# First maxima between the quarters of a feature product, and their rows sent from two queues among the last stores

## What is computed

```python
q = (x @ Wq).reshape(b, n, NUM_KV_GROUPS, GROUP_SIZE, HEAD_DIM)
k = (x @ Wk).reshape(b, n, NUM_KV_GROUPS, HEAD_DIM)
v = (x @ Wv).reshape(b, n, NUM_KV_GROUPS, HEAD_DIM)
scores = jnp.einsum('bqgsd,bkgd->bgsqk', q, k) * scale
scores = jnp.where(causal, -jnp.inf, scores)
attn = jax.nn.softmax(scores, axis=-1)
ctx = jnp.einsum('bgsqk,bkgd->bqgsd', attn, v)
```

## Time and profile before

| | |
|---|---|
| median of the runs before | 2528.2 us (2526.11 to 2528.24, 3 runs) |
| the profiled execution's own time | 2528.26 us |
| its span, first to last instruction | 2526.5 us |
| PE busy | 2413.8 us (96%) |
| DVE busy | 1737.0 us (69%) |
| ACT busy | 1426.1 us (56%) |
| POOL busy | 1610.2 us (64%) |
| mean granted PE clock | 0.972 |

### The profile page before, as it was taken

The page is one execution under the profiler, slowest core; times in us unless marked ns, Lnnn a source line. Parts: engine busy times, 40 slices in busy tenths (PEclk is TensorE's granted clock), DMA queues, the critical chain, the costliest instruction groups (busy, mean ns, idle before and its releaser), DMA issues. The chain is left out here.

```text
span 2526.5 us, 38828 instructions
## 1 busy us (share of the span) xinstructions
PE 2413.8 (96%) x12834; PEld 1726.7 (68%) x12834; DVE 1737.0 (69%) x3804; ACT 1426.1 (56%) x2761; POOL 1610.2 (64%) x1751
## 2 busy tenths in 40 slices
PE   8979999999999999996979999999999997999998
PEld 6865555555555555544767888887888885788886
DVE  3358778888888888833876655666656564877776
ACT  3215556666666666663865555666656554454553
POOL 4404577777877767776957667675576765555554
PEclk9999899999999999998989999999999998999999
DMA  7853655574656566555964545466445457674553
GB/s 248 270 169 84 132 124 125 115 151 113 145 112 145 118 144 123 116 107 157 355 202 138 166 137 159 145 217 186 152 141 160 132 164 245 189 226 131 148 151 102
DMA packets 249177, 400.87 MB, mean 159 GB/s; under 512 B 57712, under 2 KB 112016, under 8 KB 237584
## 3 DMA queue, kind: packets, MB, share of 16 engines
q1 hardware_dynamic: 196000, 283.48, 36.8%
q0 software_dynamic: 52480, 114.37, 20.5%
q10 hardware_dynamic: 496, 0.54, 0.1%
HBM read 180.63 MB, written 112.22 MB: 116 GB/s over the span
## 5 line engine op out<-in xcount | busy, mean ns | idle before, releaser
L1142 ACT ACTIVATE p_probs<-p_ps_s 128x512 f32<-128x512 f32 (+3 forms) x1280 | 591.1, 541 | 327.0 <-PE p_ps_s L1060 310.1
L1727 POOL DMA_DIRECT2D p_eT<-p_ex x1024 | 538.4, 535 | 272.9 <-DVE p_ex L1993 220.4
L1169 DVE TENSOR_REDUCE p_parts<-p_ps_m 128x1 f32<-128x512 f32 x752 | 459.1, 681 | 82.9 <-PE p_ps_m L1045 74.6
L1060 PE MATMUL p_ps_s<-q,k_e 98*128 98x512 f32 (+3 forms) x1280 | 468.4, 387 | 3.5 <-ACT p_probs L1142 3.1
L1045 PE MATMUL p_ps_m<-k_m,q 96*128 96x512 f32 (+2 forms) x1232 | 434.6, 387 | 11.9 <-PEq L2268 10.2
L981 POOL TENSOR_TENSOR p_added<-p_added,p_probs 128x2048 f32<-128x2048 f32 x88 | 419.4, 4769 | 34.5 <-ACT p_probs L1142 17.0
L1060 PEld LDWEIGHTS p_ps_s<-q,k_e 98*128 98x128 f32 x1280 | 241.8, 191 | 183.6 <-ACT p_probs L1142 76.3
L1078 PE MATMUL p_ps_c<-p_probs,v_e 128*32 128x512 f32 (+3 forms) x2560 | 285.3, 547 | 10.0 <-POOL p_probs L961 10.0
L1045 PEld LDWEIGHTS p_ps_m<-k_m,q 96*128 96x128 f32 x1232 | 235.4, 194 | 86.4 <-DVE p_parts L1173 20.2
L2127 POOL TENSOR_TENSOR p_acc<-p_acc,logit 128x512 f32<-128x512 f32 x112 | 162.5, 1451 | 153.6 <-ACT logit L2180 150.1
L1173 DVE CUSTOM_DVE_ANT_0 p_masked<-p_ps_m,p_mask 128x128 f32<-128x128 f32 (+1 forms) x480 | 203.9, 485 | 25.7 <-PE p_ps_m L1045 25.6
(11 more groups left out here) (204 smaller groups left out, 4979.4 us busy)
## 6 DMA issues: line engine op xcount, KB each, us to landing
p_probs<-p_probs POOLq DMA_DIRECT2D x56, 1024.0 KB, 7.9
logits_t<-logit SPq DMA_DIRECT2D x32, 1024.0 KB, 5.0
p_eT<-p_ex POOLq DMA_DIRECT2D x1024, 32.0 KB, 2.1
logit<-logits_t SPq DMA_DIRECT2D x128, 256.0 KB, 3.5
q<-q_t SPq DMA_DIRECT2D x96, 256.0 KB, 4.8
c_first<-L_ffn_W_dram SPq DMA_DIRECT2D x64, 256.0 KB, 5.6
p_probs<-p_probs POOLq DMA_DIRECT2D x16, 768.0 KB, 7.5
p_x<-L_attn_x_dram SPq DMA_DIRECT2D x32, 256.0 KB, 4.7
```

Of the source, the lines that this page charges most:

```text
L1060: pe.matmul(ps_s[:, u % ST_BANKS, q0:BLK], k_e[:, bass.ts(kt, P)], q[:, qb, h, q0:BLK], start=True, stop=True).then_inc(s_score, 1)
L1142: act.activation(probs[s % RING][:, h, q0:BLK], ps_s[:, u % ST_BANKS, q0:BLK], ACT.Exp).then_inc(s_exp, 1)
L1169: dve.tensor_reduce(to, bank, AX.X, ALU.max).then_inc(s_taken, 1)
L1727: pool.dma_start(eT[r][p * QD:(p + 1) * QD, i, :, :], ex[i * QD:(i + 1) * QD, 2 * r:2 * r + 2, bass.ts(p, P)]).then_inc(s_eT[r], 16)
```

## The change

The places behind which units stand become places inside products: behind every quarter (blk, m, c), from (6, 2, 0) to (7, 4, 3). These are 36 places for 48 units, so 1, 1 and 2 units in turn. The last product, (7, 5), has none behind it. On DVE the reductions of the units of a product now stand ahead of its `f_lo`, not behind it. The rows of maxima of query block 0 are sent by SP in the middle of the last block's stores (ahead of those of m = 2), those of query block 1 by ACT behind its last copy. In the attention DVE's wait for POOL's mask moves from the stage's start to the first unit that uses the mask.

```diff
-        places = [(NBLK - 2, m) for m in range(2, VT + 1)] + [(NBLK - 1, m) for m in range(VT + 1)]
-        def units_behind(blk, m):
-            if (blk, m) not in places:
+        places = [(NBLK - 2, m, c) for m in range(2, VT + 1) for c in range(DC)] + [(NBLK - 1, m, c) for m in range(VT) for c in range(DC)]
+        def units_behind(blk, m, c):
+            if (blk, m, c) not in places:
                 return []
-            at, count = places.index((blk, m)), M_END[AHEAD - 1]
+            at, count = places.index((blk, m, c)), M_END[AHEAD - 1]
...
+        def send_rows(eng, n):
+            eng.wait_ge(s_max, n + 1)
+            for a in range(4):
+                to = first[0][QROWS:MROWS, n, :, :].rearrange("o h (t a j) -> o h t a j", t=4, a=4)[:, :, :, a, :]
+                eng.dma_start(to.bitcast(F32), rows[n][a * 32:(a + 1) * 32, :]).then_inc(s_row[n], 16)
...
                 for m in range(NF):
+                    if blk == NBLK - 1 and m == 2:
+                        send_rows(sp, 0)
                     for half, src, ready, done in ((0, f_hi, s_fhi, s_ohi), (1, f_lo, s_flo, s_olo)):
...
-            for n in range(AHEAD):
-                sp.wait_ge(s_max, n + 1)
-                for a in range(4):
-                    to = first[0][QROWS:MROWS, n, :, :].rearrange("o h (t a j) -> o h t a j", t=4, a=4)[:, :, :, a, :]
-                    sp.dma_start(to.bitcast(F32), rows[n][a * 32:(a + 1) * 32, :]).then_inc(s_row[n], 16)
...
                                             xT_hi[j][:, c, :], xT_lo[j][:, c, :], c == 0, c == DC - 1)
+                        for u in units_behind(blk, m, c) if c < DC - 1 else []:
+                            unit(u)
                     last.then_inc(s_f, 1)
-                    for u in units_behind(blk, m):
+                    for u in units_behind(blk, m, DC - 1):
                         unit(u)
...
                 values(blk)
+            for n in range(1, AHEAD):
+                send_rows(act, n)
...
                 for m in ms:
+                    for c in range(DC):
+                        for u in units_behind(blk, m, c):
+                            maximum(u)
                     dve.wait_ge(s_fhi, blk * NF + (m + 1))
...
-                    for u in units_behind(blk, m):
-                        maximum(u)
...
+                    if u == FIRST_MASKED:
+                        dve.wait_ge(s_mask, 1)
                     if u - U0 >= 3:
...
-            dve.wait_ge(s_mask, 1)
             for what, a, h in order():
```

More of the change, by code:

```diff
@@ L406, in _ @@
                 features_lo(blk, range(2, NF))
-                for u in units_behind(blk, VT):
-                    maximum(u)
+                for c in range(DC):
+                    for u in units_behind(blk, VT, c):
+                        maximum(u)
             values(NBLK - 1)
@@ L434 @@
 U0 = M_END[AHEAD - 1]
+FIRST_MASKED = min(u for u in range(U0, NU) if MAXU[u][1] == BLOCKS[MAXU[u][0]][1])
 ADDED = [[], [0, 1, 3], [0, 1, 2, 3, 5, 6, 7], [0, 2, 4, 6, 7, 9, 11]]
```

## The result

| | before | after |
|---|---|---|
| median of the runs | 2527.04 us (2525.86 to 2528.24, 5 runs) | 2511.08 us (2509.46 to 2514.09, 5 runs) |
| the profiled execution's own time | 2528.26 us | 2510.2 us |
| span | 2526.5 us | 2508.5 us |
| mean granted PE clock | 0.972 | 0.975 |

The ratio is 0.9939, with a 95% interval of 0.9925 to 0.9954: faster by 15.4 us (11.6 to 19.0). I had said 2514.1 in a range from 2511.8 to 2518.5.

The account below looks back on a forecast made before the run. PE was taken as the bound, held by DVE at each group of five, then by serial row sends. (7, 5) ending 7.0 us earlier plus a shorter seam gave 14.1 us: 2528.26 - 14.1 = 2514.1, range 2511.8 to 2518.5.

Parts of the forecast that it names:

- The sum of the seam: End of projections to the attention's first matmul: (7, 5) ends 7.0 us earlier, attention starts at 177.5, 14.1 us earlier.
- 9.8 us for all 48: PE, (6, 2) to (7, 5): all spread units cost 9.0 us, plus 0.8 for narrow units standing alone.
- The way behind it: From the end of (7, 5) at 172.5 to the attention's first matmul at 177.5.
- ACT and SP: End of the stage: ACT's four row issues and SP's queue with the values' store both end at 176.0.
- "issues are slower" rival: Row transfers and stores on SP and ACT: slower issues cut the gain to 11.6 us; 0.20 shared with narrow units, landings.
- The wait behind the groups: PE, (6, 2) to (7, 5): waits of 9.0 us, PE held by DVE at each group of five; spreading removes them.
- DVE holding PE: Rival in the spread stretch: waits stay at 9.0 us as DVE is level with PE, gain 6.1 us; chance 0.05.
- a stall at each place: Rival at the 36 places on PE: with 0.5 us stalls each, 3.9 us slower, 2532.1; chance 0.03.
- wait for landings: Rival at the first `context`: a 10 us store landing cuts the gain by 1.5; 0.20 shared with slower issues, narrow units.
- The clock: Rival at the seam: PE's clock stays up or returns early, 1.7 us more gain, 2512.4; chance 0.20.
- The moved wait for the mask: Attention, DVE: costs nothing at its new place; DVE began about 0.3 us late at the old; no gain counted.
- the last one, from the seam to the time: Stages behind the seam: each starts 14.1 us earlier, unchanged, so 2528.26 becomes 2514.1; chance 0.50.

Follow-up runs that it names:

- the kernel with sends only: The kernel before with only the row transfers sent as in the changed kernel, groups and DVE's order as before: 2524.80 us, ratio 0.9990.
- the kernel spread to the last product: The changed kernel with its 48 units spread over 40 places, up to the last quarter of (7, 5): 2513.59 us in one run.

## Why the prediction was right or wrong

**The sum of the seam** was 14.1 us and measured 14.68 and 14.62. Its terms: (7, 5) was to end at 172.5 and ended at 171.92, 0.1 of it from the earlier start. The narrow single units are cheaper than I put them. I had added 0.05 to each of them; in the changed kernel one of 128 takes 0.06 us to the next matmul's start, one of 256 takes 0.12, and one of 512 takes 0.23 as in a group. So 9.8 us for all 48 was 0.5 too much. The way behind it was to be 5.0 us (172.5 to 177.5) and is 4.94.

**ACT and SP** were to end together at 176.0. ACT ended at 175.35, SP at 174.62. Two errors on ACT nearly cancel, which is luck. The four issues take 3.23 us there instead of 2.6, because the first takes 1.24; the others take about 0.64, as on SP. But the first is shown to start with the copy and not behind it, 0.6 us earlier. On SP I took the ten loads and six stores at the lengths of the earlier trace rows: the loads took 4.58 us instead of 5.45, so the row sends began at 167.70 and not 168.8, and four of the six stores behind them were 0.4 to 0.5 us long. The "issues are slower" rival was right for one issue on ACT, and wrong for SP.

**The wait behind the groups.** Here a reason failed although the number held. I wrote that PE is held by DVE at each group of five because it "asks for five within 1.2 us and has four banks", and let the reordering on DVE pass in one sentence. The runs show that most of the wait has another cause: with the reductions ahead of `f_lo` the groups of five stand idle for 0.4 us in place of 6.9, and the distance falls by 6.45 us; five units on four banks cost only the rest, some 0.4 us at a wide group. And the spread units with the reductions behind `f_lo` wait more than ever (14.5 us of idle time). The order was the cause, and the timeline of the kernel before has it, behind the group of the earlier trace rows that starts at 155.25:

```profile
155.44 0.60 ACT L320 ACTIVATE p_f_hi<-p_ps_f 128x512 fp32r<-128x512 f32 x1 [3.67 <-PE p_ps_f L75]
156.07 0.69 DVE L356 SCALAR_TENSOR_TENSOR p_f_lo<-p_ps_f,p_f_hi 128x512 fp32r<-128x512 f32 x1 [0.72 <-ACT p_f_hi L320]
```

DVE stands idle for 0.72 us until ACT has `f_hi`, while the first unit's bank is full, then does `f_lo`, and starts the first reduction at 156.68, 1.4 us behind the first unit's matmul. What the spreading itself adds is 5.15 us, most of it by having the second row ready before the last product ends.

**The rivals.** DVE holding PE, or a stall at each place, did not come. The attention did not wait for landings: the last store was issued at 174.25 and landed 3.2 us later, and the first `context` stands at 183.38. The clock was low for most of the way there in one profile of the changed kernel (a mean of 0.56, 6.52 us to the first `context`); in the other the way took 5.46 us. The moved wait for the mask shows no gain there: DVE's first reduction stands 0.80 us behind PE's first matmul instead of 0.95, and the kernel with sends only, where this wait stands as before, needed 5.55 us to its first `context`.

**The range.** The step that failed is the last one, from the seam to the time: all stages behind start "14.1 us earlier" and nothing else moves, against one execution of 2528.26 us. Of the 3.0 us between the forecast and the median of 2511.08, 1.2 are the base, whose median beside it was 2527.04 (2526.54 to 2527.54 in the three later series). Another 0.6 are the seam, and about 1.3 were won outside it. The range failed by 0.7 us because it took in only the seam's unknowns and put the other stages at nothing. Executions of the kernel before went from 2521.57 to 2534.4, those of the changed one from 2509.46 to 2515.11; low-clock periods of other stages come and go, as at 1104 us, where 2.65 us hung on one. What each of these periods costs was not measured. The range's lower end had no full path even in the seam: with ACT's issues at 0.45 us, SP's queue would still have ended at 176.0 by my own working, so the terms reach down to 2512.4, not 2511.8.

By the means of the runs the change brings 15.5 us (2527.2 over 15 executions and over 20, 2511.7 over ten), 0.9 more than the seam's 14.68. That is within the scatter, and whether some of it belongs to the changed program, for instance to the moved wait for the mask, which no run tries alone, stays open.

## What to carry to other kernels

When one engine waits for a bank and the engine that frees the bank has time to spare, look at the order on the freeing engine before moving work on the waiting one: an instruction that waits for something else at the head of its queue holds every bank behind it. Count the transfers that stand behind the last store of a stage at their issue time, whatever their size; they are paid in full when nobody else works, and a second queue or an earlier place takes them off. And end a stage's side work before its last main product, not with it.

## What was not expected of the hardware

A DMA issue on ACT is shown to start with the activation ahead of it, not behind it (172.12 both); with an explicit wait it starts at that activation's end (173.93 behind 173.30 and 0.60). The same 4 KB row transfer takes 0.60 to 0.80 us to issue on SP. On ACT most take 0.62 to 0.66 us, but the first of the four takes 1.24 to 1.27 in each of the nine profiles where ACT sends rows, whether an activation is running as it starts (172.12) or none is (174.19 in the kernel spread to the last product). Why that is so was not tried. With eight filler matmuls PE's clock fell 1.6 us into the attention although PE had been idle for 1.74 us only.
